# When the scratch fills, the first loads and the weight transposes happen in the front of a transformer layer

## What is computed

```
xn = layernorm(x)
Q, K, V = xn @ W.T + b                 # for Wq, Wk, Wv; 16 heads of 8
attn = softmax(Q K^T / sqrt(8))        # per batch and head, 512 x 512
x = x + (attn V) @ Wo.T + bo
t = layernorm(x)
logits = t @ Wr.T + br                 # top 2 of 8 experts, softmax over the two
o_e = relu(t @ W1[e].T + b1[e]) @ W2[e].T + b2[e]
x = x + layernorm(t + sum over the two of weight_e * o_e) * gamma + beta
```

## Time and profile before

| | |
|---|---|
| median of 3 runs without a profile | 710.91 us (708.14 to 712.12) |
| span of the profiled execution | 750.5 us; the page gives no time around the span |
| busy share of that span | TensorE 81%, VectorE 65%, ScalarE 60%, GpSimd 32% |
| first score | 33.78 us after the start of the span |
| first transposed score | 51.93 us |

### The profile page before, as it was taken

One profiled execution on the slowest core, in us unless ns is written; L12 is line 12 of the kernel. 1 busy time (PEld: TensorE's weight loads), 2 busy tenths in 40 slices (PEclk: granted clock), 3 DMA queues, 4 the chain that ended last, 5 costly groups with the idle time before them and its releaser, 6 DMA issues. The chain is left out here.

```text
span 750.5 us, 13269 instructions
## 1 busy us (share of the span) xinstructions
PE 609.3 (81%) x3750; PEld 321.2 (43%) x3750; DVE 489.0 (65%) x1319; ACT 447.4 (60%) x945; POOL 242.6 (32%) x454
## 2 busy tenths in 40 slices
PE   2899999879988997987987998995229998999680
PEld 1633333323333432332332333332128988888530
DVE  3579989968967985985995887751204444444357
ACT  2718888867956965875885786683114444544333
POOL 5200101150240332214115005016425665555534
PEclk9959999989998998998998899899559999999976
DMA  7552122122122122022112211000121221221193
GB/s 219 195 153 66 44 69 83 49 67 74 37 85 72 33 84 84 26 65 89 49 47 70 65 45 48 6 0 30 50 83 54 65 66 56 69 66 57 47 238 98
DMA packets 54216, 54.47 MB, mean 73 GB/s; under 512 B 8286, under 2 KB 37514, under 8 KB 54164
## 3 DMA queue, kind: packets, MB, share of 16 engines
q1 hardware_dynamic: 48372, 44.19, 20.8%
q0 software_dynamic: 4416, 8.53, 3.2%
q10 hardware_dynamic: 1376, 1.13, 0.5%
HBM read 29.01 MB, written 24.81 MB: 72 GB/s over the span
## 5 line engine op out<-in xcount | busy, mean ns | idle before, releaser
L643 DVE TENSOR_REDUCE mneg<-s_psum 128x1 f32<-128x512 f32 x512 | 325.9, 684 | 89.5 <-PE s_psum L810 55.7
L546 ACT ACTIVATE pt<-st_psum 128x512 f32<-128x512 f32 x512 | 279.9, 598 | 93.3 <-PE st_psum L826 82.7
L826 PE MATMUL st_psum<-qs,ks 64*128 64x512 f32 x512 | 202.5, 471 | 24.8 <-ACT pt L546 19.4
L810 PE MATMUL s_psum<-ks,qs 64*128 64x512 f32 x512 | 208.3, 482 | 3.3 <-DVE mneg L643 2.1
L896 PE MATMUL pv_psum<-pt,vst 128*16 128x512 f32 x1024 | 142.8, 632 | 0.0
L810 PEld LDWEIGHTS s_psum<-ks,qs 64*128 64x128 f32 x512 | 84.4, 196 | 120.2 <-DVE mneg L643 94.9
L826 PEld LDWEIGHTS st_psum<-qs,ks 64*128 64x128 f32 x512 | 82.4, 193 | 69.1 <-ACT pt L546 52.7
L1099 ACT ACTIVATE hid<-h_psum,b1c 128x256 f32<-128x256 f32 x144 | 57.2, 474 | 71.2 <-PE h_psum L1204 69.3
L1062 POOL DMA_INDIRECT results<-res,goal_now x72 | 71.6, 994 | 33.7 <-issue 33.7
L1211 PE MATMUL y_psum<-w2t,hid 128*128 128x128 f32 x576 | 73.1, 280 | 0.0
L1211 PEld LDWEIGHTS y_psum<-w2t,hid 128*128 128x128 f32 x576 | 68.9, 194 | 0.9 <-issue 0.2
(11 more groups left out here) (164 smaller groups left out, 711.3 us busy)
## 6 DMA issues: line engine op xcount, KB each, us to landing
parts<-high SPq DMA_DIRECT2D x32, 256.0 KB, 3.0
ks<-parts SPq DMA_DIRECT2D x128, 48.0 KB
qs<-parts SPq DMA_DIRECT2D x128, 48.0 KB
lot<-sent SPq DMA_DIRECT2D x37, 132.0 KB
parts<-low SPq DMA_DIRECT2D x16, 256.0 KB, 3.1
got<-results SPq DMA_DIRECT2D x16, 256.0 KB, 5.1
xres<-in_L_attn_x_dram SPq DMA_DIRECT2D x8, 256.0 KB, 3.6
pt<-in_L_ffn_W_dram SPq DMA_DIRECT2D x1, 2048.0 KB, 14.5
```

The costliest lines, as they stand in the source:

```text
L546: nc.scalar.activation(pt[:, n % PT_SLOTS, (g + 2) % 4, :], st_psum[:, k % ST_BANKS, :], ACT.Exp, scale=SCALE).then_inc(exp_done, 1)
L643: nc.vector.tensor_reduce(mneg[:, (n // 4) % 2, at:at + 1], s_psum[:, k % S_BANKS, :], AX_X, ALU.max, negate=True).then_inc(max_done, 1)
L810: mm(s_psum[:, k % S_BANKS, :], qs[rows, c, P * (n % 4):P * (n % 4) + P], ks[rows, c, g, :], start=True, stop=True).then_inc(s_made, 1)
L826: mm(st_psum[:, k % ST_BANKS, :], ks[rows, c, g, P * (n % 4):P * (n % 4) + P], qs[rows, c, :], start=True, stop=True).then_inc(st_made, 1)
```

## The change

- The weights: W1's eight groups stay in beats -8 to -5; W2's eight groups move from beats -4 to -1 to beats 0 to 3, two a beat, at the end of each beat.
- VectorE waits for `shift_done` (the scale and shift of batch 0, GpSimd's lines 384 and 386) ahead of its fills of `qs` and of quads 0 and 1 of `ks`.
- `rows_blank` becomes two semaphores, `first_blank` for VectorE's two fills and `later_blank` for ScalarE's two, and each load of batch 0 waits for the fill of its own quad.
- Quad 0's loads leave beat -6: K's go directly behind K's stores (beat -13), Q's directly behind Q's stores (beat -10). The other three quads stay in beat -6.

```diff
 def expert_weights(T):
-    return range(2 * (T + 8), 2 * (T + 8) + 2) if -8 <= T < 0 else ()
+    first = 2 * (T + 8) if -8 <= T < -4 else E + 2 * T if 0 <= T < 4 else None
+    return () if first is None else range(first, first + 2)
...
-        rows_blank, pv_blank = sem("rows_blank"), sem("pv_blank")
+        first_blank, later_blank, pv_blank = sem("first_blank"), sem("later_blank"), sem("pv_blank")
...
                 if b > 0:
                     sp.wait_ge(st_made, 16 * (q - QUADS + 1))
+                elif c < 2:
+                    sp.wait_ge(first_blank, c + 1)
                 else:
-                    sp.wait_ge(rows_blank, 4)
+                    sp.wait_ge(first_blank, 2)
+                    sp.wait_ge(later_blank, c - 1)
...
                 if (b := once(T, -13)) is not None:
                     store_parts(0, b)
+                    if b == 0:
+                        load_parts(0, 0)
                 if (b := once(T, -10 if T < 0 else -8)) is not None:
                     store_parts(1, b)
+                    if b == 0:
+                        load_parts(0, 1)
...
                 if T == -6:
-                    load_parts(0, 0)
-                    for q in range(QUADS):
+                    for q in range(1, QUADS):
+                        load_parts(q, 0)
                         load_parts(q, 1)
-                        if q + 1 < QUADS:
-                            load_parts(q + 1, 0)
...
                         nc.scalar.copy(ks[:, c], ident[:, SHIFT_ROW:P:32].unsqueeze(2).to_broadcast([P, 4, S]))\
-                            .then_inc(rows_blank, 1)
+                            .then_inc(later_blank, 1)
...
             nc.vector.memset(pv_psum[:], 0.0).then_inc(pv_blank, 1)
+            dve.wait_ge(shift_done, 1)
             nc.vector.memset(qs[:].bitcast(U32), 0)
             dve.wait_ge(ident_ready, 1)
             for c in range(2):
                 nc.vector.tensor_copy(ks[:, c], ident[:, SHIFT_ROW:P:32].unsqueeze(2).to_broadcast([P, 4, S]))\
-                    .then_inc(rows_blank, 1)
+                    .then_inc(first_blank, 1)
```

## The result

The changed kernel took 718.51 us (median of 5 runs, 716.71 to 719.0), the kernel before 710.91 beside it (5 runs, 708.14 to 713.49). The ratio on record is 1.0082, with an interval of 1.0063 to 1.0101: slower by 4.5 to 7.2 us. The two medians alone lie 7.6 apart (1.0107), a little outside that interval; five runs of the kernel before don't fix its median to better than a microsecond or two (the 24 beside the first experiments have 712.69). The forecast was 713.1 with a range to 717.0; the first rival, a clock that stays low through beats 0 to 3, had said 715.8.

The account below looks back on a forecast made before the run. The front bounds the change: beat 6 starts at the later of 52.6 (TensorE, VectorE) and 54.1 (SyncE's queue), +2.2 on 51.93; added to the median 710.91 this gives 713.1, range 707.8 to 717.0.

Parts of the forecast that it names:

- first rival: TensorE, beats 0 to 3: the clock stays low; price 4.3, beat 6 +4.9, 715.8, slower; chance 0.27.
- the forecast's mechanism: Front: SyncE's queue gates beat 6 and the clock is back by beat 2; beat 6 +2.2, 713.1; chance 0.42.
- Part 1: Start: VectorE's fills wait for the first scale; GpSimd's pow falls from 4.51 to 1.02, K's stores come 3.5 earlier.
- Part 2: K's stores on SyncE's queue: issued 3.5 earlier they still stand behind W2 and land at 23.9; no gain.
- The rule named there: Trainium skill: on each DMA engine a ring's descriptors are consumed in ring order; by it K stored at 23.9 holds.
- Part 3: Quad 0 on SyncE: Q's stores stand behind K's loads; first score at 34.4, 0.6 later.
- Part 5: SyncE's queue behind quad 0: loads end at 48.5 instead of 44.25; batch 1's shift rows +1.0 to +2.2, taken +2.2.
- part 4: Weight transposes in beats 0 to 3: clock rises at 40.5; about 1.6 lost, 1.5 back; beat 6 +0.6.
- the low beat: TensorE's beat at 1.2 GHz: four scores at 0.41, eight transposes at 0.22, 3.4 in all; VectorE needs 2.46.
- The rule about transposes: Trainium skill: transposes don't count as activity that brings the full clock; by it the first rival would hold.

Follow-up runs that it names:

- the earlier trace: The first profiled execution of the kernel before, nothing changed: profiled span 750.5 us; runs without a profile have a median of 710.91.
- the second execution: The kernel before, unchanged, profiled once more: profiled span 709.7 us, ran in 711.43 us.
- the clock held: Changed kernel plus seven 128x512 multiplications that nobody reads, on TensorE in the gap ahead of the first score: 715.28 us, ratio 1.0057.
- the fastest kernel: Changed kernel with quad 0's K loads behind Q's stores, b1, x tiles and beta behind the shift rows, three unread multiplications in TensorE's gap: 705.82 us, ratio 0.9915.

## Why the prediction was right or wrong, step by step

The time of 718.51 lies 1.5 above the range; 710.91 times the ratio, 716.7, lies just inside it. Either way the forecast's mechanism failed: what came was the first rival, which had a chance of 0.27 against 0.42. The range reaches to 717.0 only because it was drawn to take in that rival, so a time near its end owes nothing to what the forecast took for the clock and the queue.

**What held.** Part 1: pow 1.01 (1.02 foretold), K's stores at 14.29 (14.1), and the gain lost again (the run without the fills' wait). Part 2: K's stores landed 8.2 later at 23.9 (23.9), and W2 was the reason (3.0 once W2 was gone from the queue). The rule named there from the Trainium skill (DMA: Bandwidth & Descriptors, section Queues, rings and completion order) agrees with that pair, 8.2 and 3.0. Part 3: Q's stores at 26.26 (26.5), Q's loads at 30.63 (30.8), first score 33.60 (34.4), after a pause of 7.8 (8). Part 5: beta's issue at 48.06 ("near 48").

**What failed: part 4, the level of the clock.** The forecast took a rise 6.1 us after the first score, because in the earlier trace rows the clock had risen 6.1 after the weight transposes began. It rose 30.2 us after (33.60 to 63.82). The choice between forecast and first rival was the wrong one; the nearest row was not 28.36 but the stretch of the earlier trace rows from 38.60 to 55.67, in which scores, K and transposes ran low with TensorE busy for 15.85 of 17.07. That row was in hand, as the reason for the rival, and got the smaller chance.

**And its price was too small.** The rival had 4.3 for four low beats; from the first score to SHIFT it is 20.99 - 13.76 = 7.2. (By the prediction's own figures it would be 3.4 - 2.46 = 0.94 a beat and 3.8 for four; its 1.0 to 1.2 has no row.) The term that was mis-sized is the low beat: 3.4 of TensorE, made of 4 x 0.41 + 8 x 0.22. Measured are four scores in 2.30 (33.60 to 35.90) and eight transposes in 1.89 (35.90 to 37.79), together 4.19. The 0.41 was read from three scores in a row. Four are never in a row here: in beats 0 and 1 the fourth finds the three banks full and waits 0.36 for the beat's first maximum (the row at 35.18), which itself starts 0.83 after the first score; in beats 2 and 3 they run two by two, at 0.57 each (41.99 to 43.14). That is 0.8 a beat more. Beats 2 and 3 add 1.05 and 2.0 for the xn transposes and K of batch 1, and two scores of beat 4 stand ahead of SHIFT (1.16): 4 x 4.19 + 1.05 + 2.0 + 1.16 = 20.97. In a low beat TensorE is then the bound, not VectorE, so all of it shows: TensorE was busy for 20.27 of 20.99.

**Part 5's queue did not bind.** The forecast let it decide, with +2.2. K of batch 1 is multiplied in beat 3; with the slow beats its low part was ready only at 53.2, when SyncE had been done with beta since 49.75. The row of 53.19 starts the moment K is ready: the shift rows landed at 58.2 because the beats were slow, not because the queue was. Where the beats are not slow, the queue does bind: 2.98 with the weights back, 4.74 with the clock held.

**So the sum.** With the measured terms the first rival is 33.60 + 20.99 + 3.78 = 58.37 for beat 6, 6.4 behind the 51.93 of the earlier trace rows and 6.65 behind the second execution; 710.91 + 6.65 = 717.6, against 718.51 measured. Between the profiled spans 7.5 lie: 6.7 at the 65th maximum, 1.4 more up to the last one (464.06 against 455.89), which is one more long batch (last section), and 0.6 less behind it.

**The rule about transposes.** The Trainium skill (TensorE: Matmul & The Clock Gate, section Part 4: PE-mode transpose) would have given the rival, and the clock stayed low as the rival has it; but the runs do not bear the rule out as its cause. In the changed kernel the clock was first recorded in full at 22.86, in the middle of the W1 transposes, as at 28.36 before. With the clock high before the first score, the same mix of scores and transposes kept it (1.00 over 33.55 to 46.19). And in the kernel before it is low from 39.08 on with no weight transposes in the beats. So neither mix is bound to a level. In the two pairs of runs in which only the pause ahead of the first score differs (20.99 against 12.64, 20.98 against 12.64), beats 0 to 3 kept the level at which the first score found the clock: low after 7.8 or 2.84 us without work, and then for 34 or 31 us in all; high after 1.27 or 1.36 us. Without the transposes in the beats it fell all the same, 2.7 to 5.9 us behind a first score that had found it high (the fills' wait alone, the kernel before).

Not settled: why the low level lasted until 63.82 with TensorE busy nearly all the time. The moved transposes are not needed for it: with the weights back it lasted 27.3 us, with the fills' wait alone 30.7. No run was made to vary the mix of work inside the low stretch.

## What to carry to other kernels

Work taken from ahead of a gate leaves a pause there, and here 2.84 us of pause on TensorE went with 31 us at the low clock. What that costs depends on the work that lies in it: from the first score to SHIFT it took 12.64 at the high clock with eight transposes a beat, 14.06 at the low one without them, and 20.99 at the low one with them. When you cost a move, cost the beats at the low level as the default and ask for a row that shows a rise out of the very same mix of work. At the low level read a price from the pattern in which the instructions will stand (behind full banks, two by two), not from the longest run of them. When two gates lie close together (clock and queue here), removing one shows the other: undone singly, the causes gave back 0.3% to 0.7%, none enough for a kernel faster than before, and of these only the load order's 0.7% is clear of the intervals; together, with the x tiles later, it was 1.7%, part of it outside the front. And read a gain some beats behind the gate too: with the clock held, 3.3 us at beat 6 were 0.4 at beat 16.

## What the runs showed of the hardware

**A batch of the attention has two durations in these runs.** In the second execution of the kernel before the batch from 134.09 takes 53.19 at a clock of 1.00 throughout (its row above). The changed kernel's batch takes 54.76, with the clock at 0.50 from 156.0 to 159.4; the table by stretches:

```profile
140.82:195.58 54.76, 51.62 (x322) 20.28 (x320) 48.00 (x115) 43.51 (x90) 16.53 (x32) 0.97 0.24 70
...
156.00:159.40 3.40, 3.40 (x15) 1.06 (x16) 1.60 (x3) 1.23 (x4) 2.06 (x10) 0.50 0.49 168
```

VectorE and ScalarE do the same work in both, so 1.5 us is what one such stretch costs. In the profiled executions it came in every batch from some batch on: in five of the changed kernel, four of the kernel before (second execution), three of the fastest; the first execution of the kernel before is longer still, 61.4. One batch fewer is the 1.4 us that the fastest kernel gained on the kernel before where no line differs. What sets the first such batch was not tried; at 1.5 us each they matter where half a per cent is asked for.

**Small work on GpSimd and VectorE's fills stretch each other.** The pow took 4.51 beside the fills, 1.01 without them. Moved, the fills only meet other work: behind the pow VectorE's two casts lie beside GpSimd's small memsets and took 3.24 instead of the 2.29 of the earlier trace rows, while one such memset of 128x2 took 1.06 instead of 0.10.

**Before its first record the granted clock is unknown.** The table by stretches prints 1.00 for 15.00 to 22.86, where twelve transposes took 2.82 and twelve later ones 1.88; the durations tell the level there, the column does not.
